# Outer dimensions of two kinds of head copies in an attention and MoE kernel: query rows in 24, 24 and 8, skewed bias rows 32 by 3

## The chip, the cores and the metric

The kernel runs on one core of one Trainium2 chip. The metric is the device time of one execution in microseconds (us). The five compute engines are TensorE (PE; PEld is its weight load), VectorE (DVE), ScalarE (ACT), GpSimd (POOL) and SyncE (SP), which here only issues DMA transfers and waits for semaphores. The core's transfers run on 16 DMA engines.

## The reference, cut to what matters

Two attention blocks in a row and a mixture of experts, on 2 sequences of 1024 tokens with 128 features, 16 heads of 8. The first attention block adds a bias that depends only on the distance i - m (a table of 2L - 1 numbers per head):

```python
q, k, v = (heads(q_), heads(k_), heads(v_))
bias = tisa_bias(kernel_offsets, kernel_amplitudes, kernel_sharpness, l)   # scores[:, i - j + l - 1]
logits = jnp.einsum('bhld,bhmd->bhlm', q, k) * scale + bias[None]
out = jnp.einsum('bhlm,bhmd->bhld', softmax(logits), v)
```

The second one (`_msa`) is the same without the bias, with other weights and after a layer norm. Then come a projection, a top-1 choice among 8 experts and the expert's two matrices.

## The kernel before, in words

**Units.** A stage (0: with the bias, 1: without) is 32 units, a unit being one head of one sequence, 1024 x 1024 scores. Each unit is computed twice. Form A (`block_a`, L1110) has the queries on the partitions, 8 blocks of 128 x 1024; DVE takes each row's maximum, in stage 0 with the bias added from a table in SBUF (L831), in stage 1 without (L834). Form B (`scores_b`, L1166) has the keys on the partitions, so that the exponential (ACT, L693) can go straight into the product with v (`weigh_v`, L1118). The negated maxima enter form B as three more rows of its operand. In stage 0 the bias enters form B through matmuls with a flip matrix (`bias_b`, L1173), which turns around and sums 96 shifted copies of the head's bias row: three bf16 parts by 32 shifts. Form A runs two units ahead of form B (AU = 2), woven into it on PE.

**Operands.** The float32 numbers of q and k are kept as three bf16 parts. q_parts and k_parts lie in DRAM; for each head `rows_of` (L385) copies 56 rows of q and 56 of k (the products of parts that count) into a ring of four head slots, once for each half of the partitions (f = 0, 1). A q copy (L392) reads the same 24 rows twice into 48 partitions; its source has the outer dimension 2. A k copy reads 16 rows, each three times; its source has the outer dimension 16. Eight more rows follow each (L394). `skew_of` (L332, issued at L336) copies the 96 shifted bias rows of a head; its source has the outer dimension 3. `table_of` (L326, L330) copies the bias table of form A, 64 rows at a time.

**The way of the maxima.** For each unit: DVE maxima of 8 blocks, split by POOL into three parts (L561), transposed by PE (L1147), copied by DVE into max_rows (L841), stored by SP to DRAM (`maxima_of`, L418: 24 rows, 6 KB), and after the store has landed loaded as 3 rows into the q ring (L422, two transfers). PE waits for these loads (`mrow_loaded`, L1195) ahead of the unit's first form B block. All of this is SP's queue, written by hand in `stage` (L425): per unit the table, the maxima of the next unit, then at an even unit the skewed copies of the next head (L440) and the q rows of a head to come (L446), at an odd unit its k rows. In the first 8 units of stage 1 two transfers of expert weights follow each (L406, L407).

**Start of a stage.** `first_rows` (L397) stores the parts of sequence 0, loads head 0's rows of it, stores those of sequence 1, waits until all stores have landed (L383) and loads the rest; then come head 1's rows (L413). In stage 0 ACT issues the skewed copies of heads 0 and 1 (L680) meanwhile.

Of the kernel before, what the change touches and what calls it, by code (L numbers as in the profile page):

```python
# [6 lines left out]
def sandwich_kernel(nc, x, w_in, offsets, amplitudes, sharpness, ln1_w, ln1_b, w_qkv, w_proj,  # L7
# [16 lines left out]
    B, L, D = x.shape  # L24
    P = 128
    T = B * L
# [3 lines left out]
    DH = D // H  # L30
    SCALE = float(np.float32(1.0) / np.sqrt(np.float32(DH)))
    EPS = 1e-5
    E, _, HID = w1.shape
    HC = HID // P
    U = B * H
# [5 lines left out]
    PAIRS = H // 2  # L41

    KR = 7 * DH
    QK_DMAS = 8
    HP = P // 2
    UB = 8
    TAW = 2 * L - P
    SKW = 2 * L - 32
# [17 lines left out]
    with ExitStack() as ctx:  # L66
# [265 lines left out]
        def skew_of(queue, h, slot):  # L332

            row = bp_dram[bass.ds(h, 1), 0, 0:SKW]
            src = bass.AP(row.tensor, row.offset, [[2 * L, 3], [1, 32], [1, SKW]])
            queue.dma_start(skew[0:96, slot, 0:SKW], src).then_inc(skew_loaded[slot], 16)  # L336

        ctx.enter_context(nc.allow_non_contiguous_dma(reason="head rows and skewed tables"))
# [4 lines left out]
        def _(sp):  # L343
# [41 lines left out]
            def rows_of(a, h, slot, loaded, which=(0, 1), lo=0, hi=T):  # L385
                for s in which:
                    ring = (q_ring, k_ring)[s][slot]
                    one = (qp_dram, kp_dram)[s][a][bass.ds(h, 1), 0, 0, lo:hi]
                    pairs = ([[0, 2], [T, 3 * DH]], [[T, 2 * DH], [0, 3]])[s]
                    last = (qp_dram[a][bass.ds(h, 1), :, 0, lo:hi], kp_dram[a][bass.ds(h, 1), 2, :, lo:hi])[s]  # L390
                    for f in range(2):
                        sp.dma_start(ring[f * HP:f * HP + 6 * DH, lo:hi],  # L392
                                     bass.AP(one.tensor, one.offset, pairs + [[1, hi - lo]])).then_inc(loaded, 16)
                        sp.dma_start(ring[f * HP + 6 * DH:f * HP + KR, lo:hi],  # L394
                                     last.rearrange("o d n -> (o d) n")).then_inc(loaded, 16)

            def first_rows(a):  # L397

                store_parts(a, range(G // 2))
                rows_of(a, 0, 0, first_loaded[a], lo=0, hi=L)  # L400
                store_parts(a, range(G // 2, G))
                rows_of(a, 0, 0, qk_loaded[a][0], lo=L, hi=T)
# [8 lines left out]
            sp.wait_ge(ones_ready, 1)  # L411
            first_rows(0)
            rows_of(0, 1, 1, qk_loaded[0][1])  # L413
            def maxima_of(a, u, ul):

# [63 lines left out]
        def _(pool):  # L479
            steps = [0]  # L480

            def chain(ins):

                steps[0] += 1
                ins.then_inc(pool_step, 1)
                pool.wait_ge(pool_step, steps[0])
# [6 lines left out]
                                          pattern=[[-1, P]], channel_multiplier=1))  # L493
# [5 lines left out]
                                          pattern=[[P, 2], [-NK, VM]], channel_multiplier=1))  # L499
            nc.gpsimd.affine_select(out=amp_sel[:], in_=amp_sel[:], compare_op=ALU.is_ge, fill=0.0,  # L500
                                    base=NK - 1, pattern=[[-P, 2], [NK, VM]], channel_multiplier=-1).then_inc(mask_ready, 1)
# [9 lines left out]
            chain(nc.gpsimd.memset(flip[:], 0.0))  # L511
            for n in range(3):
                chain(nc.gpsimd.affine_select(out=flip[:], in_=flip[:], compare_op=ALU.not_equal, fill=1.0,
                                              base=-31 - 32 * n, pattern=[[1, 32]], channel_multiplier=1))
            pool.sem_inc(flip_ready, 1)

            nc.gpsimd.iota(order[:], [[-1, E]], base=E, channel_multiplier=0,
# [6 lines left out]
                                          pattern=[[1, P]], channel_multiplier=-1))  # L524
# [3 lines left out]
                                          pattern=[[1, E], [-1, E]], channel_multiplier=0))  # L528
# [95 lines left out]
        def _(act):  # L624
# [54 lines left out]
            for h in range(2):  # L679
                skew_of(act, h, h)  # L680
# [364 lines left out]
        def _(pe):  # L1045
# [90 lines left out]
            def block_a(a, u, ul, qb, guard, halves=(0, 1)):  # L1136

                if guard:
                    pe.wait_ge(max_done[a], QB * u + qb - 1)
                for f in halves:  # L1140
                    ins = scores_a(qb % 2, (ul // B) % 4, ul % B, qb, f)
                return ins
# [34 lines left out]
            def stage(a):  # L1177
                for qb in range(QB):
                    if qb == 0:
                        pe.wait_ge(first_loaded[a], 16 * QK_DMAS)  # L1180
                    block_a(a, 0, 0, qb, qb >= 2).then_inc(sa_done[a], 1)
                pe.wait_ge(qk_loaded[a][0], 16 * QK_DMAS)
                for qb in range(QB):
# [6 lines left out]
                def body(i, first=False, last=False):  # L1190
                    for ul in range(UB):
# [6 lines left out]
                        for kb in range(QB):  # L1198
                            if kb == 0 and lu % B == 0 and not done:
                                pe.wait_ge(qk_loaded[a][(lu // B) % 4], 16 * QK_DMAS * (i + 1 + lu // UB))  # L1200
                            for f in range(2):
# [180 lines left out]
```

## Time and profile before

| | |
|---|---|
| Three runs, median (lowest to highest) | 1099.91 us (1099.27 to 1103.8) |
| The profiled execution, its own time | 1094.4 us |
| Its span, from the first to the last instruction | 1092.3 us |
| PE, DVE, ACT busy | 80%, 71%, 59% of the span |
| Mean granted TensorE clock | 0.906 of full speed (2.4 GHz) |
| DMA: mean rate, reads from HBM | 66 GB/s, 59.95 MB |
| Chain that ended last, by engine | PE 49%, DMA 20%, DVE 9%, ACT 8% |

The span is divided so: the start until about 93 us; stage 0's units until about 558 us; layer norms and projections until about 609 us; stage 1's units until about 968 us; the mixture of experts to the end. The chain is the chain of waits that ended last, followed back from the end: a share of it that belongs to a transfer is time in which nothing else on the chain could go on.

### The profile page before, as it was taken

How to read it: one execution, taken by the hardware profiler on the slowest of the kernel's cores; microseconds unless marked ns; L12 is line 12 of the kernel's file. 1: busy time of each engine (PE TensorE's matmuls, PEld its weight loads, DVE VectorE, ACT ScalarE, POOL GpSimd, SP SyncE). 2: the span in 40 equal slices, each digit the busy share in tenths (PEclk: the TensorE clock that was granted, in tenths of full speed). 3: DMA queues.
4: the chain of work that ended last, by engine and by line, in shares of the span. 5: the costliest groups of instructions: out<-in, count | busy, mean ns of one | idle time of the engine just before them, and what ended most of it. 6: DMA issues, size and time to landing. Idle time of an engine off the chain costs nothing.

```text
span 1092.3 us, 25373 instructions
## 1 busy us (share of the span) xinstructions
PE 870.8 (80%) x9075; PEld 327.7 (30%) x9075; DVE 771.5 (71%) x1388; ACT 641.3 (59%) x1208; POOL 138.9 (13%) x376
## 2 busy tenths in 40 slices
PE   3328979998998999989946387999979999984871
PEld 2102323333332333323313011222322222243861
DVE  7356757776775777767358676899969999746544
ACT  6204646665665666656646066889869889941222
POOL 8100000000000000000010000000100100001772
PEclk9757989999998999999978588999989999996996
DMA  2722223233223223320002323321111110001123
GB/s 56 215 75 74 75 73 86 83 86 87 67 71 80 86 84 84 84 78 24 3 1 62 122 57 89 110 82 48 54 37 48 58 44 30 3 1 48 43 48 89
DMA packets 41965, 72.18 MB, mean 66 GB/s; under 512 B 9177, under 2 KB 28825, under 8 KB 41849
## 3 DMA queue, kind: packets, MB, share of 16 engines
q1 hardware_dynamic: 40018, 65.81, 21.3%
q0 software_dynamic: 1472, 3.02, 1.1%
q10 hardware_dynamic: 358, 1.76, 0.5%
q8 instruction: 79, 1.29, 0.5%
q14 instruction: 38, 0.30, 0.1%
HBM read 59.95 MB, written 10.62 MB: 65 GB/s over the span
## 4 chain that ended last, share of the span: by engine, by line
PE 49%; DMA 20%; DVE 9%; ACT 8%; issue 6%; SPq 4%; POOL 3%; DVEq 0%; ACTq 0%; POOLq 0%
PE bank L1118 16%; DMA maxima_rows<-max_rows 13%; PE bank L1166 13%; PE bank L1173 9%; ACT prob_mem L693 7%; PE bank L1110 6%; DVE unit_max L834 2%; DMA k_parts<-prob_mem 2%; POOL moe_out L616 2%; DMA q_rows<-maxima_rows 2%; DVE stats L750 2%; POOL prob_mem L605 1%; DVE norm L764 1%; SPq L392 1%; SPq L373 1%
## 5 line engine op out<-in xcount | busy, mean ns | idle before, releaser
L693 ACT ACTIVATE prob_mem<-bank 128x512 f32<-128x512 f32 x1024 | 555.3, 597 | 317.7 <-PE bank L1173 232.4
L831 DVE CUSTOM_DVE_ANT_0 y_res<-bank,tables 128x1024 bf16<-128x1024 f32 x256 | 312.3, 1224 | 158.6 <-PE bank L1110 149.5
L834 DVE TENSOR_REDUCE unit_max<-bank 128x1 f32<-128x1024 f32 x256 | 294.7, 1214 | 40.1 <-PE bank L1110 39.9
L1118 PE MATMUL bank<-prob_mem,v_ring 128*32 128x256 f32 x4096 | 315.2, 394 | 2.3 <-issue 1.7
L1110 PE MATMUL bank<-k_rows,q_rows 56*128 56x512 bf16 x512 | 164.0, 425 | 57.9 <-DMA k_rows<-k_parts 43.6
L1166 PE MATMUL bank<-q_rows,k_rows 59*128 59x512 bf16 x512 | 170.3, 401 | 44.8 <-DMA q_rows<-maxima_rows 26.2
L1166 PE MATMUL bank<-more_rows 59*128 59x512 bf16 x512 | 162.3, 389 | 28.2 <-DMA more_rows<-maxima_rows 15.1
L1173 PE MATMUL bank<-feat,flip 96*32 96x512 bf16 x2048 | 163.9, 395 | 0.0
L1110 PE MATMUL bank<-more_rows 56*128 56x512 bf16 x512 | 162.7, 392 | 0.0
L1118 PEld LDWEIGHTS bank<-prob_mem,v_ring 128*32 128x32 f32 x4096 | 107.1, 111 | 150.1 <-ACT prob_mem L693 58.7
L561 POOL CAST max_parts<-unit_max 128x8 bf16<-128x8 f32 x64 | 12.2, 191 | 809.6 <-DVE unit_max L831 463.5
L1166 PEld LDWEIGHTS bank<-q_rows,k_rows 59*128 59x128 bf16 x512 | 39.1, 94 | 167.7 <-ACT prob_mem L693 74.3
L1166 PEld LDWEIGHTS bank<-more_rows 59*128 59x128 bf16 x512 | 39.3, 93 | 147.9 <-ACT prob_mem L693 76.0
L1110 PEld LDWEIGHTS bank<-k_rows,q_rows 56*128 56x128 bf16 x512 | 36.8, 95 | 73.2 <-issue 27.2
L1173 PEld LDWEIGHTS bank<-feat,flip 96*32 96x32 bf16 x2048 | 32.3, 95 | 75.0 <-issue 75.0
L727 ACT ACTIVATE prob_mem<-bank 128x512 f32<-128x512 f32 x23 | 13.8, 598 | 67.5 <-PE bank L1327 67.5
L1110 PEld LDWEIGHTS bank<-more_rows 56*128 56x128 bf16 x512 | 37.6, 94 | 0.3
L815 DVE RECIPROCAL recip<-bank 128x8 f32<-128x8 f32 x64 | 12.0, 187 | 34.2 <-PE bank L1104 34.2
L605 POOL DMA_INDIRECT prob_mem<-tokens,gather_u x23 | 24.8, 1078 | 59.9 <-DVE gather_u L970 53.2
L1104 PE MATMUL bank<-ident,o_ring 128*128 128x128 f32 x128 | 28.2, 302 | 0.9 <-ACT o_ring L670 0.5
L1327 PE MATMUL bank<-prob_mem 128*128 128x128 f32 x184 | 27.2, 294 | 0.0
L670 ACT COPY o_ring<-bank 128x256 f32<-128x256 f32 x64 | 24.3, 379 | 4.9 <-PE bank L1118 4.7
(159 smaller groups left out, 565.4 us busy)
## 6 DMA issues: line engine op xcount, KB each, us to landing
tables<-bias_rows SPq DMA_DIRECT2D x30, 480.0 KB, 8.5
more_rows<-q_parts SPq DMA_DIRECT2D x32, 192.0 KB
more_rows<-k_parts SPq DMA_DIRECT2D x32, 192.0 KB
q_rows<-q_parts SPq DMA_DIRECT2D x28, 192.0 KB
k_rows<-k_parts SPq DMA_DIRECT2D x28, 192.0 KB
feat<-bias_parts SPq DMA_DIRECT2D x14, 378.0 KB
w_moe<-in_L_ffn_w_dram SPq DMA_DIRECT2D x16, 256.0 KB, 3.8
q_parts<-prob_mem SPq DMA_DIRECT2D x8, 384.0 KB, 3.2
```

The lines of the kernel that those rows point to most:

```text
L605: nc.gpsimd.indirect_dma_start(out=slot_rows[:, j % 4, :], out_offset=None, in_=tokens_dram, in_offset=bass.IndirectOffsetOnAxis(ap=gather ...
L616: nc.gpsimd.indirect_dma_start(out=moe_dram, out_offset=bass.IndirectOffsetOnAxis(ap=token_u[:, j:j + 1], axis=0), in_=slot_y[:, j, :], in ...
L670: nc.scalar.copy(o_ring[:, slot, :], AV).then_inc(o_ready[a], 1)
L693: nc.scalar.activation(prob[:, ul % 2, kb, half * N:(half + 1) * N], b_bank(entry(ul, kb, half)), ACT.Exp).then_inc(exp_done[a], 1)
L831: nc.vector.tensor_tensor_reduce(out=no_use[qb % 2], in0=scores, in1=bias, scale=1.0, scalar=LEAST, op0=ALU.add, op1=ALU.max, accum_out=un ...
L834: nc.vector.tensor_reduce(unit_max[:, slot, qb:qb + 1], scores, AX.X, ALU.max).then_inc(max_done[1], 1)
L1104: ins = nc.tensor.transpose(out[:, half * P:(half + 1) * P], o_ring[:, slot, half * P:(half + 1) * P], ident[:])
L1110: return nc.tensor.matmul(SA[slot][:, f, :], q_ring[head_slot][rows, b * L + qb * P:b * L + (qb + 1) * P], k_ring[head_slot][rows, b * L + ...
L1118: ins = nc.tensor.matmul(AV[VM * c:VM * (c + 1), :], v_ring[:, head_slot, b * QB + kb, :], prob[:, ul % 2, kb, c * W:(c + 1) * W], start=( ...
L1166: return nc.tensor.matmul(b_bank(entry(ul, kb, f)), k_ring[ul // B][rows, b * L + kb * P:b * L + (kb + 1) * P], q_ring[ul // B][rows, b * ...
L1173: ins = nc.tensor.matmul(b_bank(entry(ul, kb, f))[32 * c:32 * (c + 1), :], flip[:], skew[0:96, (ul // B) % 2, at:at + N], start=False, sto ...
L1327: ins = nc.tensor.matmul(bank[:, 2 + n % 2, c * P:(c + 1) * P], w_ring[:, n, c * P:(c + 1) * P], slot_feat[:, n, :], start=True, stop=True)
```

## The change

The copies move the same bytes from the same rows to the same partitions, apart from the skewed bias.

- A q copy of 48 rows from a source of 2 by 24 rows is now two copies of 24 rows, whose source has the outer dimension 24. The copy of 8 rows stays (outer dimension 8). A head's rows are therefore 10 transfers and not 8 (`QK_DMAS`).
- The skewed copies read 32 by 3 and not 3 by 32 rows: partition 3 i + n now holds shift i of part n, where partition 32 n + i did. It is one transfer as before.
- The flip matrix has its ones where the new partitions want them.

```diff
-    QK_DMAS = 8
+    QK_DMAS = 10
...
             row = bp_dram[bass.ds(h, 1), 0, 0:SKW]
-            src = bass.AP(row.tensor, row.offset, [[2 * L, 3], [1, 32], [1, SKW]])
+            src = bass.AP(row.tensor, row.offset, [[1, 32], [2 * L, 3], [1, SKW]])
             queue.dma_start(skew[0:96, slot, 0:SKW], src).then_inc(skew_loaded[slot], 16)
...
-                    pairs = ([[0, 2], [T, 3 * DH]], [[T, 2 * DH], [0, 3]])[s]
                     last = (qp_dram[a][bass.ds(h, 1), :, 0, lo:hi], kp_dram[a][bass.ds(h, 1), 2, :, lo:hi])[s]
                     for f in range(2):
-                        sp.dma_start(ring[f * HP:f * HP + 6 * DH, lo:hi],
-                                     bass.AP(one.tensor, one.offset, pairs + [[1, hi - lo]])).then_inc(loaded, 16)
+                        if s == 0:
+                            for r in range(2):
+                                sp.dma_start(ring[f * HP + 3 * DH * r:f * HP + 3 * DH * (r + 1), lo:hi],
+                                             bass.AP(one.tensor, one.offset, [[T, 3 * DH], [1, hi - lo]])).then_inc(loaded, 16)
+                        else:
+                            sp.dma_start(ring[f * HP:f * HP + 6 * DH, lo:hi],
+                                         bass.AP(one.tensor, one.offset, [[T, 2 * DH], [0, 3], [1, hi - lo]])).then_inc(loaded, 16)
...
-                                              base=-31 - 32 * n, pattern=[[1, 32]], channel_multiplier=1))
+                                              base=-93 - n, pattern=[[3, 32]], channel_multiplier=1))
```

How SP's queue stands at an even unit of stage 0 (more_rows and q_rows are slots of the q and k rings, feat holds the skewed copies). Before:

```order
L418 DMA maxima_rows<-max_rows 24x128
L422 DMA q_rows<-maxima_rows 3x512 x2
L336 DMA feat<-bias_parts 96x1x2016
L392 DMA q_rows<-q_parts 48x1x2048
L394 DMA q_rows<-q_parts 8x2048
L392 DMA q_rows<-q_parts 48x1x2048
L394 DMA q_rows<-q_parts 8x2048
L330 DMA tables<-bias_rows 64x1920
L418 DMA maxima_rows<-max_rows 24x128
```

And with the change (its file has four more lines, so L418 is L422 there):

```order
L422 DMA maxima_rows<-max_rows 24x128
L426 DMA q_rows<-maxima_rows 3x512 x2
L336 DMA feat<-bias_parts 96x1x2016
L393 DMA q_rows<-q_parts 24x2048 x2
L398 DMA q_rows<-q_parts 8x2048
L393 DMA q_rows<-q_parts 24x2048 x2
L398 DMA q_rows<-q_parts 8x2048
L330 DMA tables<-bias_rows 64x1920
L422 DMA maxima_rows<-max_rows 24x128
```

Between two stores of maxima SP issues two more transfers, with the same neighbours. SP's queue at the start of a stage, from the first half of head 0's rows to the second. Before:

```order
L392 DMA q_rows<-q_parts 48x1x1024
L394 DMA q_rows<-q_parts 8x1024
L392 DMA q_rows<-q_parts 48x1x1024
L394 DMA q_rows<-q_parts 8x1024
L392 DMA k_rows<-k_parts 48x1x1024
L394 DMA k_rows<-k_parts 8x1024
L392 DMA k_rows<-k_parts 48x1x1024
L394 DMA k_rows<-k_parts 8x1024
L369 DMA q_parts<-prob_mem 384x1x512
L373 DMA k_parts<-prob_mem 16x8x512 x3
```

And with the change:

```order
L393 DMA q_rows<-q_parts 24x1024 x2
L398 DMA q_rows<-q_parts 8x1024
L393 DMA q_rows<-q_parts 24x1024 x2
L398 DMA q_rows<-q_parts 8x1024
L396 DMA k_rows<-k_parts 48x1x1024
L398 DMA k_rows<-k_parts 8x1024
L396 DMA k_rows<-k_parts 48x1x1024
L398 DMA k_rows<-k_parts 8x1024
L369 DMA q_parts<-prob_mem 384x1x512
L373 DMA k_parts<-prob_mem 16x8x512 x3
```

Here too there are two more q transfers ahead of the k rows and ahead of the stores that follow; nothing else changes its place.

## Rows read from the trace of the kernel before

**Rows 1.** The page, part 4: the chain of waits by line.

```profile
PE bank L1118 16%; DMA maxima_rows<-max_rows 13%; PE bank L1166 13%; PE bank L1173 9%; ACT prob_mem L693 7%; PE bank L1110 6%; DVE unit_max L834 2%; DMA k_parts<-prob_mem 2%; POOL moe_out L616 2%; DMA q_rows<-maxima_rows 2%; DVE stats L750 2%; POOL prob_mem L605 1%; DVE norm L764 1%; SPq L392 1%; SPq L373 1%
```

**Rows 2.** Chain of waits, stage 0: start us, us, what.

```profile
257.30 8.79 DMA maxima_rows<-max_rows
...
266.40 1.44 DMA more_rows<-maxima_rows
```

**Rows 3.** PE in order of time, the unit after that store: start, us, instruction, idle before.

```profile
268.16 0.38 PE L1166 MATMUL bank<-more_rows 59*128 59x512 bf16 x1 [2.55 <-DMA more_rows<-maxima_rows]
```

**Rows 4.** Windows there: stretch, us, busy per engine, PEclk, DMA share, GB/s.

```profile
256.00:264.00 8.00, 7.48 (x99) 2.62 (x97) 6.00 (x12) 4.85 (x10) 0.00 (x0) 1.00 0.13 53
...
269.00:271.00 2.00, 2.00 (x18) 0.51 (x12) 1.23 (x2) 1.09 (x2) 0.00 (x0) 0.50 0.79 185
```

**Rows 5.** SP in order of time, issues of that head: start, us to issue, transfer.

```profile
245.90 0.81 SPq L336 DMA_DIRECT2D feat<-bias_parts  x1
246.93 0.69 SPq L392 DMA_DIRECT2D q_rows<-q_parts  x1
...
250.20 0.54 SPq L330 DMA_DIRECT2D tables<-bias_rows  x1
257.30 0.31 SPq L418 DMA_DIRECT2D maxima_rows<-max_rows  x1
...
275.09 0.31 SPq L418 DMA_DIRECT2D maxima_rows<-max_rows  x1
276.39 0.56 SPq L422 DMA_DIRECT2D more_rows<-maxima_rows  x2
```

**Rows 6.** DMA of 511 to 523 us, a skewed copy alone: GB/s in 40 slices of 0.3 us.

```profile
GB/s 0 0 3 7 10 0 0 27 13 27 54 81 81 81 81 81 81 81 135 81 81 81 81 81 67 54 0 0 0 0 0 0 0 0 27 0 27 0 0 0
```

**Rows 7.** SP in order of time, stores of the maxima in stage 0.

```profile
122.00 0.30 SPq L418 DMA_DIRECT2D maxima_rows<-max_rows  x1
...
318.69 0.31 SPq L418 DMA_DIRECT2D maxima_rows<-max_rows  x1
...
339.09 0.31 SPq L418 DMA_DIRECT2D maxima_rows<-max_rows  x1
...
496.30 0.30 SPq L418 DMA_DIRECT2D maxima_rows<-max_rows  x1
...
509.76 0.29 SPq L418 DMA_DIRECT2D maxima_rows<-max_rows  x1
...
523.23 0.30 SPq L418 DMA_DIRECT2D maxima_rows<-max_rows  x1
```

**Rows 8.** PE in order of time, first instruction of stage 0's unit 16.

```profile
330.94 0.60 PE L1166 MATMUL bank<-q_rows,k_rows 59*128 59x512 bf16 x1 [3.55 <-issue]
```

**Rows 9.** Chain of waits, start of stage 0.

```profile
50.46 16.44 DMA k_parts<-prob_mem
...
79.29 5.93 DMA maxima_rows<-max_rows
```

**Rows 10.** Windows of the start of stage 0, columns as in rows 4.

```profile
50.00:52.00 2.00, 0.00 (x0) 0.00 (x0) 0.00 (x0) 0.00 (x0) 0.00 (x0) 0.50 1.06 363
...
52.00:58.00 6.00, 2.80 (x10) 0.47 (x10) 4.13 (x7) 0.00 (x0) 0.00 (x0) 0.50 0.26 91
58.00:64.00 6.00, 1.88 (x8) 0.31 (x6) 5.12 (x10) 0.00 (x0) 0.56 (x4) 0.50 0.19 75
```

**Rows 11.** SP in order of time, stage 1.

```profile
633.73 0.29 SPq L418 DMA_DIRECT2D maxima_rows<-max_rows  x1
...
641.80 0.42 SPq L407 DMA_DIRECT2D w_moe<-in_L_ffn_w_dram  x1
...
740.43 0.30 SPq L418 DMA_DIRECT2D maxima_rows<-max_rows  x1
...
750.18 0.30 SPq L418 DMA_DIRECT2D maxima_rows<-max_rows  x1
```

**Rows 12.** Chain of waits, stage 1, a store of maxima in its first units.

```profile
645.12 6.95 DMA maxima_rows<-max_rows
```

## The prediction

> **What bounds the kernel now.** I read the page first: the chain of waits by line. Among the matmuls stands a transfer, the store of the maxima, with 13% of the span, more than any other transfer [rows 1]. It moves 6 KB, so its time is a wait behind something. Next the chain in time: the store issued at 257.30 lands after 8.79 us, its load takes 1.44 us more [rows 2], and PE, which stood idle for 2.55 us, starts the unit at 268.16 [rows 3]. The store after it, issued at 275.09, lets SP go on at 276.39, after 1.30 us [rows 5]. So the same store takes 1.3 us on an empty queue and 8.8 on a full one.
>
> What fills the queue is seen in the windows. From 256 to 264 us the DMA engines are 13% busy and move 53 GB/s [rows 4]: 0.13 of 16 is two engines, 27 GB/s each. What was issued before were the skewed copies and the q rows of a head [rows 5]. Where the skewed copy runs alone, the rate stands at 81 GB/s from 514.3 to about 518.5 us, slice after slice [rows 6]: three engines of 27. Two is the outer dimension of the q copy's source and three that of the skewed copy's. So a copy here runs on as many engines as its source has outer entries, and the store, some of whose rows go through the same engines, waits until these two or three have finished, while 13 stand idle. Per head the two busiest get 378/3 = 126 KB of skewed rows, 2 x 192/2 = 192 KB of q rows, and some 40 KB of the 8-row copies and the table: about 360 KB, 13.5 us at 27 KB per us. From 247 us on that is 260.5, and later while the table shares them; the landing was at 266.1.
>
> The last piece is the price of the stall. PE has no slack in stage 0: with nothing in the way a unit takes 13.47 us (509.76 to 523.23) [rows 7]. After the idle time the granted clock is 0.50, the lower of the two levels (1.2 GHz), in the window from 269 to 271 us [rows 4]. The stall of 2.55 us plus the slow matmuls make the step 257.30 to 275.09 17.8 us long [rows 5], 4.3 above a clean one.
>
> **The change part by part.** The sum is made against the profiled execution's 1094.4 us (its span of 1092.3 and 2.1 around it).
>
> *1. Stage 0's units, gain 29 us.* From the store at 122.00 to that at 496.30 lie 25 units in 374.3 us [rows 7]; at 13.47 they would take 336.8. The excess is 37.5 us. Ahead of unit 16, the first after the loop's back edge, PE is idle for 3.55 us and waits for nothing that the profile shows ("issue") [rows 8]; that step, 318.69 to 339.09 [rows 7], is 6.9 over, and I leave all of it. That leaves 30.6 in twelve heads, all in the units after a heavy burst. With the change the burst (378 + 448 + 480 = 1306 KB, the table among it) is spread. The nearest rate for such copies on all engines is the 185 GB/s at 0.79 share of k rows and table [rows 4]: 7.1 us from 247, done by 255, before the store at 257.3. The store then lands in 1.3 us, as at 275.09. PE was ready for the unit 2.55 us before 268.16, at 265.6 [rows 3], so store and load may take 8.3 us together; they would take some 3.3. Even at half the rate the burst ends at 261 and PE doesn't wait. I take 29 of the 30.6, for the odd step that stays long. Bounds: 0 (nothing spreads) and 31.
>
> *2. Start of stage 0, gain 10 us.* The last store of k parts, issued at 50.46, takes 16.44 us [rows 9], and SP waits for it. From 50 to 52 us all engines are busy at 363 GB/s, but from 58 to 64 us only 0.19 of them, again three, at 75 [rows 10]: ACT's two skewed copies, 252 KB on each of three engines, and then two engines of q rows. What was still to move after 52 us is the 546 and 450 KB of the two windows behind it and a rest, about 1.1 MB; at between 185 and 363 GB/s that is 3 to 6 us, so the store lands at about 58.5 and not at 66.9, 8.4 us earlier (two more q issues ahead of it, 1.4 us, are in that). Unit 1's rows are issued next: two more q issues cost 1.4 us there, and rows that spread land sooner by about as much (96 KB of 2-KB rows on each of two engines were 3.6 us at 27 KB per us): net nothing. The maxima's first store, 5.93 us [rows 9], falls to about 1.5; DVE's maxima of unit 1 then end last, and about 2 us of the 4.4 show. 8.4 + 2 = 10.4, taken as 10. Bounds 3 and 13.
>
> *3. Start of stage 1, loss 1 us.* There no skewed copy lies in the way, and the stores of the parts wait for SP's own issuing. Two more in each half of the rows cost 4 x 0.69 [rows 5] = 2.8 us; shorter landings give back about 1.8. Bounds: loss 3, gain 2.
>
> *4. Stage 1's first units, gain 13 us.* A clean unit takes 9.75 us (740.43 to 750.18). From 633.73 to 740.43 there are nine in 106.7 us [rows 11], 18.9 over nine clean ones. The store at 645.12 takes 6.95 us there [rows 12]. The q rows (192 KB on each of two engines, 7.3 us) are the tail of each burst at an even unit. With q, k and two expert transfers spread evenly, 1.4 MB or so, the burst takes some 7.6 us at 185 GB/s, about what SP takes to issue it, and the store behind it lands in 2 to 3 us. Some of the excess is the low clock after the stage's start. I take 13. Bounds 5 and 18. Later stage 1 steps are clean already: nothing.
>
> *5. Issue cost, nothing in the loops.* 0.69 us for each of two more transfers per head [rows 5], 1.4 us. In stage 0 SP is done with the table at 250.7 and waits for the maxima until 257.30 [rows 5]: 6.6 us of cover. In stage 1's first units it ends at 642.22 [rows 11] with the next store at 645.12 [rows 12]: 2.9. Only there would a shorter unit (9.75) bring SP near the path. The flip matrix costs nothing: the same three POOL instructions at the start, the same 32 columns for PE.
>
> One rule bears on how far a 24-row copy spreads, for which no row stands; the rates above bound it between two engines and all, and I take many, by the fit of both rates to the outer dimension. The Trainium skill (DMA: Bandwidth & Descriptors, in the section on why a DMA increments its semaphore by 16 and not by 1) says that a DMA takes the largest number up to 16 that divides the slowest dimensions of both sides: 2 and 3 here before, as the trace agrees with 54 and 81 GB/s, and 12 and 16 with the change; 12 or 16 makes no difference to the sum. No copy with 24 outer entries is seen alone in this trace.
>
> Sum: 29 + 10 - 1 + 13 = 51 us, 1094.4 - 51 = 1043.4. The three runs' median is 5.5 above the profiled execution; a measurement is compared with the median, so I give 1099.9 - 51 = 1048.9, or 1049. The sum's bounds together (0 and so on up, but hardly all at one end) give 1037 to about 1075.
>
> **The rivals.**
>
> *A. The q rows stay on few engines, only the skewed copies spread.* This would come from the two 24-row copies running one behind the other on the same engines, so that splitting wins nothing. For it: no row shows a 24-row q copy. Against it: the rates fit the outer dimension twice. Then engines 0 and 1 have 360 - 126 + 24 = 258 KB, 9.6 us from 247: free by about 257 to 259, and the store still lands in time, so term 1 stays at 27. Term 2 falls to 7, term 4 to 0, term 3 to -3: 1099.9 - 31 = 1069. The Trainium skill has a rule that points this way (same page, Rules for kernel authors: two transfers to disjoint partition halves serialize, so one should not bother). Its reason is that both halves already use all 16 engines, which the 53 GB/s of the before trace denies here. Chance 0.1.
>
> *B. The reads of the skewed copies collide.* Its 96 rows overlap, shifted by 2 bytes, and 16 engines would read the same few kilobytes at once. The table, also overlapping, is among what moves at 185 GB/s, half of the 363 seen elsewhere. If the skewed copy alone fell to some 50 GB/s it would take 7.6 us and the burst about 13, until 260: the stalls shrink but some stay. Term 1 then gives 20, term 2 gives 5: 1099.9 - 37 = 1063. Chance 0.09.
>
> *C. Slower: SP's issuing becomes the path.* The place is the queue between the loads of the maxima (L422) and the next store (L418). If the split copies cost much more to issue than 0.69 us (queue space, 24 entries over more engines), the store starts late in every even unit. It decides from 6.6 us more per head in stage 0 and about 3 in stage 1; at 4 us an issue (two more, and four dearer) stage 1 would lose some 10 us per head, 100 us, against 40 gained: 1160. Even at a mild 2 us an issue stage 1 loses about 3 x 16 = 48 and the result is 1050 + 60 = 1110. Against it: the table copy, with 2.5 times the bytes of a q copy, costs 0.54 us and not more [rows 5]. Chance 0.03.
>
> *D. No change.* The spread copies reach the store just as late, since the sum of bytes and not the two engines is the limit: 1306 KB would have to take over 13 us, below 100 GB/s. The 185 GB/s of the nearest window speaks against it. 1098. Chance 0.03.
>
> **How the numbers follow.** My forecast has 0.75, A 0.1, B 0.09, C 0.03, D 0.03. The forecast, A and B are all faster by more than 0.5% (5.5 us, about what a measurement of this kernel can tell from no change): 0.94. D is 0.03, C 0.03. The range holds the time 8 times in 10: from 1036, where all terms of the forecast come near their upper bounds (31 + 13 + 0 + 18 = 62, 1038), to 1072, which takes in A and B.
>
> **What would show it right or wrong.** In the profile after: the chain's share of the maxima's store falls from 13% to 2 or 3%; the steps between stores in stage 0 are all 13.4 to 13.6 us but for unit 16; right after a skewed copy the windows show a share above 0.7 for 5 to 7 us and none at 0.13; the mean granted clock rises above 0.93; the k parts' store at the start takes 7 to 9 us and not 16.4; stage 1's first stores of the maxima land within 3.5 us. It is wrong if the 0.13 windows stay (A), if a window with the skewed copy alone shows a high share at a low rate (B), or if the store is issued late behind SP's other transfers (C). If the stores land quickly but the steps stay at 15 us or more, PE's stall had another cause and the theory of terms 1 and 4 falls.

## The result and the profile after

The changed kernel takes 1032.59 us (median of 4 runs, 1031.16 to 1035.85) against 1099.59 (1097.62 to 1103.8): a ratio of 0.939, 95% interval 0.9354 to 0.9426, 67 us less. The forecast was 1049, with 1036 as the low end. So the sign and the mechanism were right and the size was not: a quarter of the gain wasn't foreseen.

The profiled execution has a span of 1030.0 us (before 1092.3) and a mean granted clock of 0.923 (before 0.906). The chain by line on the page of the changed kernel, which answers to [rows 1] (its line numbers are four higher from L418 on):

```profile
PE bank L1122 21%; PE bank L1170 16%; PE bank L1177 13%; ACT prob_mem L697 10%; PE bank L1114 7%; PE bank L1341 1%; PE bank L1331 1%; PE bank L1108 1%; DVE stats L754 1%; DVE norm L768 1%; DVE unit_max L838 1%; DMA prob_mem<-tokens,gather_u 1%; ACT o_ring L674 1%; DVE meanvar L757 1%
```

The maxima's store, 13% of the chain before, is gone from the list. SP's queue at an even unit of stage 0, in order of time (start us, us to issue), which answers to [rows 5]:

```profile
133.54 0.30 SPq L422 DMA_DIRECT2D maxima_rows<-max_rows  x1
134.84 0.55 SPq L426 DMA_DIRECT2D more_rows<-maxima_rows  x2
135.44 0.58 SPq L336 DMA_DIRECT2D feat<-bias_parts  x1
136.06 1.52 SPq L393 DMA_DIRECT2D q_rows<-q_parts  x2
...
139.05 0.51 SPq L330 DMA_DIRECT2D tables<-bias_rows  x1
147.01 0.30 SPq L422 DMA_DIRECT2D maxima_rows<-max_rows  x1
```

And the windows over it (stretch, us, busy per engine, PEclk, DMA share, GB/s), which answer to [rows 4]:

```profile
137.00:139.00 2.00, 2.00 (x32) 0.75 (x24) 1.72 (x3) 1.57 (x4) 0.00 (x0) 1.00 0.85 245
139.00:141.00 2.00, 2.00 (x28) 0.67 (x28) 1.50 (x4) 1.39 (x3) 0.00 (x0) 1.00 0.86 195
141.00:143.00 2.00, 2.00 (x36) 0.80 (x28) 1.65 (x3) 1.25 (x3) 0.45 (x3) 1.00 1.00 160
143.00:145.00 2.00, 2.00 (x30) 0.71 (x24) 1.72 (x3) 1.63 (x4) 0.30 (x2) 1.00 0.22 46
145.00:147.00 2.00, 1.50 (x17) 0.45 (x15) 1.71 (x6) 1.34 (x4) 0.00 (x0) 1.00 0.00 0
```

The same bytes go through in some 8 us, most of them with nearly all engines busy, and nothing is left when the store is issued at 147.01; before, two engines worked on for 8 us more. The skewed copy alone, on the changed kernel from 466 to 478 us (GB/s in 40 slices of 0.3 us, and the issue), answers to [rows 6]:

```profile
GB/s 0 0 0 10 10 0 0 134 81 202 390 390 94 0 0 0 0 55 0 0 0 0 0 0 0 0 0 0 0 0 0 0 0 0 0 27 0 27 0 0
...
feat<-bias_parts SPq DMA_DIRECT2D x1, 378.0 KB, 3.6
```

What took over 4 us at 81 GB/s now takes some 1.8 us (six slices) with 390 GB/s at its height. The stores of stage 0, which answer to [rows 7]:

```profile
106.61 0.30 SPq L422 DMA_DIRECT2D maxima_rows<-max_rows  x1
...
282.46 0.31 SPq L422 DMA_DIRECT2D maxima_rows<-max_rows  x1
...
302.71 0.31 SPq L422 DMA_DIRECT2D maxima_rows<-max_rows  x1
...
451.56 0.29 SPq L422 DMA_DIRECT2D maxima_rows<-max_rows  x1
```

From the fourth store to the 29th it is 344.95 us, before 374.3. The step 282.46 to 302.71 is the one at the loop's back edge, 20.25 us as before (20.40). Of the other 24 steps 22 are 13.40 to 13.47 us and two 14.25. The start, which answers to [rows 9]:

```profile
58.59 0.72 SPq L393 DMA_DIRECT2D q_rows<-q_parts  x2
...
69.14 0.30 SPq L422 DMA_DIRECT2D maxima_rows<-max_rows  x1
70.79 0.92 SPq L426 DMA_DIRECT2D q_rows<-maxima_rows  x2
...
80.25 0.29 SPq L422 DMA_DIRECT2D maxima_rows<-max_rows  x1
```

SP goes on from the stores of the parts at 58.59, before at 66.9; the first maxima go out at 69.14, before at 79.29, and SP goes on to their loads after 1.65 us and not 5.95. Last stage 1, which answers to [rows 11], with the last store of all:

```profile
575.64 0.30 SPq L422 DMA_DIRECT2D maxima_rows<-max_rows  x1
585.06 0.29 SPq L422 DMA_DIRECT2D maxima_rows<-max_rows  x1
...
673.73 0.30 SPq L422 DMA_DIRECT2D maxima_rows<-max_rows  x1
683.49 0.30 SPq L422 DMA_DIRECT2D maxima_rows<-max_rows  x1
...
885.30 0.29 SPq L422 DMA_DIRECT2D maxima_rows<-max_rows  x1
```

The places to compare in the kernel before are these (the others stand in [rows 7] and [rows 11]):

```profile
621.10 0.30 SPq L418 DMA_DIRECT2D maxima_rows<-max_rows  x1
...
952.37 0.29 SPq L418 DMA_DIRECT2D maxima_rows<-max_rows  x1
```

So the span's 62.3 us divide: to the fourth store 122.00 - 106.61 = 15.4; stage 0's 25 steps 29.4; from there to stage 1's first store (621.10 and 575.64) 124.8 - 124.1 = 0.7; the next ten steps (621.10 to 740.43 against 575.64 to 673.73) 119.3 - 98.1 = 21.2; the rest of stage 1 0.4; and from the last store to the end it is 144.7 against 139.9, 4.8 us lost.

Of the signs that the prediction named, the stall's all came: the store has left the chain, the steps of stage 0 are clean, and SP waits at most 2.5 us for a store of the maxima in stage 1's first ten steps. One didn't: the mean granted clock was to rise above 0.93 and is 0.923. In the changed kernel it is 0.99 from 107 to 452 us and 0.98 from 674 to 885 us; most of what is left of the slow clock lies ahead of the units (0.80 until 69 us), between the stages (0.83) and behind the last store (0.82), where the change does little.

### The profile page after: what moved, and what is told of

It is laid out like the page before. It is cut to its first block, busy times and chain, and to the rows that moved or that the text cites. A ratio compares the mean times of both kernels' runs of the same rounds, so it can differ in the third digit from the quotient of the medians.

```text
span 1030.0 us, 25473 instructions
## 1 busy us (share of the span) xinstructions
PE 859.8 (83%) x9075; PEld 329.0 (32%) x9075; DVE 769.7 (75%) x1388; ACT 640.3 (62%) x1208; POOL 138.8 (13%) x376
## 3 DMA queue, kind: packets, MB, share of 16 engines
q10 hardware_dynamic: 384, 1.76, 0.6%
q8 instruction: 78, 1.28, 0.5%
## 4 chain that ended last, share of the span: by engine, by line
PE 64%; ACT 12%; DVE 6%; issue 5%; DMA 2%; SPq 1%; another core or an unknown queue 1%; POOL 1%; DVEq 0%; ACTq 0%; POOLq 0%
PE bank L1122 21%; PE bank L1170 16%; PE bank L1177 13%; ACT prob_mem L697 10%; PE bank L1114 7%; PE bank L1341 1%; PE bank L1331 1%; PE bank L1108 1%; DVE stats L754 1%; DVE norm L768 1%; DVE unit_max L838 1%; DMA prob_mem<-tokens,gather_u 1%; ACT o_ring L674 1%; DVE meanvar L757 1%
## 5 line engine op out<-in xcount | busy, mean ns | idle before, releaser
L1122 PE MATMUL bank<-prob_mem,v_ring 128*32 128x256 f32 x4096 | 310.0, 388 | 2.5 <-issue 2.0
L1170 PE MATMUL bank<-q_rows,k_rows 59*128 59x512 bf16 x512 | 167.4, 395 | 18.5 <-ACT prob_mem L697 8.9
L1170 PE MATMUL bank<-more_rows 59*128 59x512 bf16 x512 | 159.5, 384 | 12.7 <-ACT prob_mem L697 9.4
L1177 PE MATMUL bank<-feat,flip 96*32 96x512 bf16 x2048 | 161.1, 389 | 0.0
L1114 PE MATMUL bank<-more_rows 56*128 56x512 bf16 x512 | 158.7, 382 | 0.0
L1331 PE MATMUL bank<-prob_mem 128*128 128x128 f32 x184 | 28.4, 304 | 6.6 <-issue 6.0
L1341 PE MATMUL bank<-prob_mem 128*128 128x128 f32 x184 | 26.4, 290 | 4.2 <-issue 2.3
```

The costliest lines, as they stand in the source:

```text
L1114: return nc.tensor.matmul(SA[slot][:, f, :], q_ring[head_slot][rows, b * L + qb * P:b * L + (qb + 1) * P], k_ring[head_slot][rows, b * L + ...
L1122: ins = nc.tensor.matmul(AV[VM * c:VM * (c + 1), :], v_ring[:, head_slot, b * QB + kb, :], prob[:, ul % 2, kb, c * W:(c + 1) * W], start=( ...
L1170: return nc.tensor.matmul(b_bank(entry(ul, kb, f)), k_ring[ul // B][rows, b * L + kb * P:b * L + (kb + 1) * P], q_ring[ul // B][rows, b * ...
L1177: ins = nc.tensor.matmul(b_bank(entry(ul, kb, f))[32 * c:32 * (c + 1), :], flip[:], skew[0:96, (ul // B) % 2, at:at + N], start=False, sto ...
L1331: ins = nc.tensor.matmul(bank[:, 2 + n % 2, c * P:(c + 1) * P], w_ring[:, n, c * P:(c + 1) * P], slot_feat[:, n, :], start=True, stop=True)
L1341: ins = nc.tensor.matmul(bank[:, 4 + n % 2, 0:D], hidden[:, n % 2, c, :], w_ring[:, n, HID + c * D:HID + (c + 1) * D], start=(c == 0), sto ...
```

## The experiments

"Theory T" is the prediction's: a copy runs on as many engines as its source has outer entries, and the maxima's store waits for the busiest of the engines that it shares. The rivals are S (what counts is into how many transfers the q rows are cut) and what the expectations call theory B (the skewed copies are all of it; not the rival B of the prediction). Kernels that were timed together share their runs of the kernel before: its median is 1102.77 us for e1 to e4 and 1102.54 for e6, e7, e9 and e10.

**e1, the skewed copies alone.** The q copies are as before.

```diff
-            src = bass.AP(row.tensor, row.offset, [[2 * L, 3], [1, 32], [1, SKW]])
+            src = bass.AP(row.tensor, row.offset, [[1, 32], [2 * L, 3], [1, SKW]])
...
-                                              base=-31 - 32 * n, pattern=[[1, 32]], channel_multiplier=1))
+                                              base=-93 - n, pattern=[[3, 32]], channel_multiplier=1))
```

> The skewed copies read 32 by 3 rows, the q copies stay as in the kernel before (48 rows, outer dimension 2). Theory T (a copy runs on as many engines as its source has outer entries; the maxima's store waits for the busiest of its engines): with the skewed rows spread, engines 0 and 1 carry about 258 KB per head, 9.6 us, and are free at about the time of the store, so stage 0's units between its fourth and 29th store come close to the changed kernel (345 to 352 us where before has 374), the start gains about 8 us, stage 1's first units gain nothing (ten steps 119 us, as before). Sum about 35 us: 1060 to 1068. Theory S (the number of transfers into which the q rows are cut is what counts, not the engines): no gain beyond a few us, 1090 or more. Theory B (the skewed copies are all of it, q nothing): 1033.

Measured: 1072.04 us (1066.33 to 1072.69), ratio 0.9698 (0.9633 to 0.9762). Stage 0 is nearly as clean as with the whole change:

```profile
113.57 0.30 SPq L418 DMA_DIRECT2D maxima_rows<-max_rows  x1
...
465.02 0.29 SPq L418 DMA_DIRECT2D maxima_rows<-max_rows  x1
...
589.70 0.30 SPq L418 DMA_DIRECT2D maxima_rows<-max_rows  x1
...
711.03 0.30 SPq L418 DMA_DIRECT2D maxima_rows<-max_rows  x1
```

351.45 us for the 25 steps, 6.5 more than with the change, all of it in the first two (16.39 and 17.14). The two stores there take 9.51 and 8.62 us. Ahead of the first, q and k rows of a head are issued in one unit (from 105.73 us on); ahead of the second, SP, held up by the first, issues the skewed copy and the q rows only from 123.69 on, 6.3 us before the store. Stage 1's first ten steps take 121.3 us, nothing gained. There the windows show the two engines again:

```profile
616.00:618.00 2.00, 2.00 (x28) 0.53 (x24) 2.00 (x2) 1.96 (x5) 0.00 (x0) 1.00 0.13 51
```

Both are what T says; the total is 4 us above its range. S, which expected 1090 or more, and B, which expected 1033, both miss.

**e2, the q copies alone.** The skewed copies and the flip matrix are as before.

```diff
-            src = bass.AP(row.tensor, row.offset, [[1, 32], [2 * L, 3], [1, SKW]])
+            src = bass.AP(row.tensor, row.offset, [[2 * L, 3], [1, 32], [1, SKW]])
...
-                                              base=-93 - n, pattern=[[3, 32]], channel_multiplier=1))
+                                              base=-31 - 32 * n, pattern=[[1, 32]], channel_multiplier=1))
```

(against the changed kernel)

> The q copies as in the change, the skewed copies and the flip matrix as before (outer dimension 3). T: three engines carry about 126 + 56 KB and more of k, 7 us per head, so stage 0's units are as with the whole change (345 us from the fourth store to the 29th); at the start ACT's two skewed copies still hold three engines for 9.4 us, and the last k parts store lands at about 62 us (66.9 before, 58.6 with the change); stage 1 is as with the change (98 us for ten steps). 1034 to 1042. If the skewed copies were needed too, stage 0 would stay above 360 us and the time above 1048. B: 1090 or more.

Measured: 1035.96 us (1035.65 to 1036.36), ratio 0.9385 (0.9329 to 0.9441).

```profile
58.25 0.71 SPq L393 DMA_DIRECT2D q_rows<-q_parts  x2
...
74.08 0.30 SPq L422 DMA_DIRECT2D maxima_rows<-max_rows  x1
...
113.28 0.30 SPq L422 DMA_DIRECT2D maxima_rows<-max_rows  x1
...
458.29 0.29 SPq L422 DMA_DIRECT2D maxima_rows<-max_rows  x1
```

345.01 us in stage 0 and 98.55 for stage 1's ten steps: as the whole change. The one thing off is the start. The parts' stores let SP go on at 58.25, not at 62 as expected, and the loss comes later, where unit 1's rows are loaded: the first maxima go out 15.8 us after that, with the whole change 10.6. Theory B falls: the q copies alone give nearly all of the gain. The two halves of the change don't add up: against the same runs of the kernel before they gain 31 and 67 us alone, and both together 70 to 72 (e3 and e4 below, which are the changed kernel). In stage 0 removing either burden is nearly enough (351.45 and 345.01 us for the 25 steps, with both removed 344.95, before 374.3).

**e3 and e4, meant as outer dimension 2 and 8.**

```diff
-                                             bass.AP(one.tensor, one.offset, [[T, 3 * DH], [1, hi - lo]])).then_inc(loaded, 16)
+                                             bass.AP(one.tensor, one.offset, [[12 * T, 2], [T, 12], [1, hi - lo]])).then_inc(loaded, 16)
```

(e4: `[[3 * T, 8], [T, 3], [1, hi - lo]]`)

> The changed kernel, but each 24-row q copy reads its rows as 2 by 12: same bytes, same number of transfers as the change, outer dimension 2. T: the q rows are back on two engines, so this is as the skewed copies alone (e1), 1060 to 1070, with windows at 0.13 DMA share and about 54 GB/s in stage 1. S: splitting is what counts, 1033. The issue of a copy: if a third dimension makes it dear, a 24-row copy takes about 0.6 us and not 0.35.

> The changed kernel, but each 24-row q copy reads its rows as 8 by 3: outer dimension 8. T: eight engines carry 48 KB each of a head's q rows, under 2 us, so nothing waits: 1033, or up to 1037 if three dimensions make each issue 0.6 us and not 0.35 (eight such issues more or dearer at each start of a stage, about 1 us per half of the rows). S: 1033. If only 12 or more engines would do, 1040 and more.

Measured: 1031.16 us (1029.05 to 1032.87), ratio 0.9346 (0.9289 to 0.9404), and 1032.59 (1032.35 to 1038.88), ratio 0.9372 (0.9309 to 0.9435). Taken at its word e3 would have ended T. Their traces agree: two of their q copies are mostly issued in 0.70 to 0.72 us, as in the change, where e6's take some 1.3 to 1.5. One thing is worth reading in them, the windows from 80 to 86 us, first of the changed kernel:

```profile
80.00:86.00 6.00, 5.90 (x76) 2.12 (x80) 3.92 (x9) 3.67 (x7) 0.00 (x0) 1.00 0.36 95
```

and of e4, the same program:

```profile
80.00:86.00 6.00, 6.00 (x50) 1.67 (x48) 2.47 (x4) 2.18 (x5) 0.00 (x0) 0.53 0.32 94
```

At the granted clock of 0.53, close to the lower level, e4's second step takes 15.78 us, that of the changed kernel 13.26. The difference is one between executions of the same program, not one that the change makes.

**e6, a true outer dimension of 2.**

```diff
-                                             bass.AP(one.tensor, one.offset, [[T, 3 * DH], [1, hi - lo]])).then_inc(loaded, 16)
+                                             bass.AP(one.tensor, one.offset, [[T, 2], [2 * T, 12], [1, hi - lo]])).then_inc(loaded, 16)
```

 Here each 24-row q copy reads the even rows and then the odd ones, 2 by 12, which can't be merged: outer dimension 2, the same two transfers per half as the change, skewed copies spread. Its q rows stand in another order than the k rows, so the scores are other numbers; all work is the same. T (engines by outer dimension): as e1, 1062 to 1075, ten first steps of stage 1 near 121 us where the change has 98, windows at 0.13 share there. S (splitting is what counts): 1031 to 1036.

Measured: 1072.34 us (1071.95 to 1074.03), ratio 0.9733 (0.968 to 0.9785), the time of e1. Stage 1's first ten steps take 120.9 us. A window, a store in the chain of waits, and SP's issue of two of the new copies:

```profile
620.00:622.00 2.00, 2.00 (x24) 0.43 (x20) 2.00 (x3) 1.95 (x5) 0.00 (x0) 1.00 0.13 52
```

```profile
631.67 8.80 DMA maxima_rows<-max_rows
```

```profile
608.36 1.34 SPq L393 DMA_DIRECT2D more_rows<-q_parts  x2
```

The q rows are cut into just as many transfers as in the change, and all of q's gain is gone. S falls. (The scores that e6, e7 and e10 compute are other numbers than the kernel's; behind their last store they take 144.2 to 146.1 us, e1 145.4, so the difference lies in the units.)

**e7, one transfer of 48 rows with outer dimension 24.**

```diff
-                            for r in range(2):
-                                sp.dma_start(ring[f * HP + 3 * DH * r:f * HP + 3 * DH * (r + 1), lo:hi],
-                                             bass.AP(one.tensor, one.offset, [[T, 3 * DH], [1, hi - lo]])).then_inc(loaded, 16)
+                            sp.dma_start(ring[f * HP:f * HP + 6 * DH, lo:hi],
+                                         bass.AP(one.tensor, one.offset, [[T, 3 * DH], [0, 2], [1, hi - lo]])).then_inc(loaded, 16)
```

(and `QK_DMAS = 8`)

> One q copy of 48 rows per half as before (8 transfers per head), but its source is 24 rows, each read twice in a row: outer dimension 24, inner 2. The q rows stand in another order than the k rows, so the scores are other numbers. Skewed copies spread. T: as the change, 1030 to 1036, since only the outer dimension matters. S: as e1, 1062 to 1075. Issue cost: if it goes with the rows of a copy and not with its number of engines, 0.6 to 0.7 us, as two of 24.

Measured: 1034.08 us (1031.9 to 1035.56), ratio 0.9376 (0.9324 to 0.9428): the changed kernel's. Stage 1's first ten steps take 98.2 us. The window and the issue:

```profile
622.00:624.00 2.00, 2.00 (x25) 0.47 (x18) 2.00 (x3) 2.00 (x6) 0.98 (x5) 1.00 1.00 242
```

```profile
610.43 0.84 SPq L392 DMA_DIRECT2D q_rows<-q_parts  x1
```

With e6 this is the decisive pair: split and outer dimension 2 gains nothing, unsplit and outer dimension 24 gains all. The further dimension in the source, which e6 and e7 both have, is no explanation either.

**e10, outer dimension 4.** As e6 with `[[T, 4], [4 * T, 6], [1, hi - lo]]`.

> As e6, but 4 by 6 rows: outer dimension 4, the q rows in another order than k's. T: four engines carry 96 KB each per head, 3.6 us and not 7.3; of what e6 loses in stage 1's first ten steps (about 23 us) at most a third is left, stage 0 as the change: 1033 to 1043, and above all between e7 and e6. S: 1031 to 1036.

Measured: 1043.76 us (1043.32 to 1045.47), ratio 0.9473 (0.9423 to 0.9524); ten steps take 102.0 us, and a store there in the chain is

```profile
615.20 5.15 DMA maxima_rows<-max_rows
```

So stage 1's first ten steps are 120.9, 102.0 and 98.2 us with 2, 4 and 24 outer entries. An outer dimension of 4 leaves a sixth of the loss. That these copies run on four engines is inferred from this; no window shows them alone. The total is 1 us above the range expected. Of its 9.4 us over e7's profile 3.8 lie in these ten steps, 2.8 and 2.5 at the starts of the stages and 2.2 behind the loop's back edge in stage 0, and 1.9 come back behind the last store; whether the dearer issues cause those outside the ten steps wasn't tried apart.

**e9, e11, e12, e14: what the start is worth.** ACT's two skewed copies and head 1's table are issued early and stand ahead of the parts' stores. e9 issues them when head 0's rows have landed:

```diff
-            for half in range(2):
-                table_of(act, 1, 1, half)
             act.wait_ge(bias_parts_stored, 16 * 4)
+            act.wait_ge(qk_loaded[0][0], 16 * QK_DMAS)
             for h in range(2):
                 skew_of(act, h, h)
+            for half in range(2):
+                table_of(act, 1, 1, half)
```

> The changed kernel, but ACT issues the two skewed copies and then head 1's table only when head 0's rows have all landed. T for the start: the last k parts store waits behind whatever is in the queues (1.7 MB of tables and skewed rows before it), so it lands 3 to 5 us earlier than at 58.6 and the first maxima's store goes out 2 to 5 us earlier than at 69.1; the skewed rows are still there when form B wants them: 1028 to 1031 against 1032.6. Rival: unit 0's and 1's blocks on DVE set the start, and the late skewed copies are waited for: 1033 to 1037.

Measured: 1037.71 us (1033.53 to 1040.02), ratio 0.9401 (0.9345 to 0.9456).

```profile
52.89 0.71 SPq L393 DMA_DIRECT2D q_rows<-q_parts  x2
...
63.35 0.30 SPq L422 DMA_DIRECT2D maxima_rows<-max_rows  x1
74.57 0.92 SPq L426 DMA_DIRECT2D q_rows<-maxima_rows  x2
...
83.28 0.29 SPq L422 DMA_DIRECT2D maxima_rows<-max_rows  x1
```

The stores land 5.7 us earlier and the first maxima go out 5.8 us earlier, but these now wait 11.2 us behind tables and skewed rows. The theory of the expectation, an earlier end, falls. The time is 0.7 us above the rival's range, but neither of the rival's reasons is what the trace shows: DVE's blocks don't hold up the first store (it goes out 5.8 us earlier), and PE waits 9.35 us for the load of the maxima, not for the skewed copies. The bytes that were put later came back on the maxima's store. e11 keeps the table early and has only the skewed copies wait for the parts' stores; e12 puts the table behind the first maxima's loads:

```diff
             act.wait_ge(bias_parts_stored, 16 * 4)
+            act.wait_ge(parts_stored[0], 16 * 4 * G)
             for h in range(2):
                 skew_of(act, h, h)
```

> The changed kernel, but ACT issues its two skewed copies only when all stores of the parts have landed; head 1's table stays early. In e9 the stores landed at 52.9 and not at 58.6, but table and skewed rows together then held up the first maxima's store by 11.2 us. Theory (the stores wait for the bytes ahead of them): 0.76 MB less ahead of them, so they land at 55 to 57, the first maxima's store goes out 2 to 3 us earlier than at 69.1 and still lands in 2 to 3 us: 1029 to 1032 against 1032.6. Rival (any byte put later comes back on the maxima's store): 1032 to 1036.

> As e11, and head 1's table is issued only when the first maxima have been loaded. Theory: stores land at about 53, the first maxima's store goes out at about 63.5 and lands in 2 to 3 us, form B starts about 5 us earlier; the table is there when form A's unit 2 wants it (it takes about 4 us): 1026 to 1030. Rival: DVE waits for the table, or the clock's rise later than with the change takes the gain: 1031 to 1036.

Measured, on another chip on which the kernel before takes 1092.59 us: 1024.51 (1023.16 to 1026.59), ratio 0.9389 (0.9353 to 0.9425), and 1026.03 (1024.9 to 1029.48), ratio 0.9406 (0.9369 to 0.9443). The times look better than the change, the ratios don't. So both were set side by side: the changed kernel (e13) and e11 again (e14).

> The changed kernel itself beside e14 on one chip, since kernels timed on different chips can't be compared within 1% (before took 1102.5 and 1092.6 us in the last two comparisons). 0.935 to 0.942 of before.

> e11 again, beside the changed kernel. If the earlier stores are worth anything at the end, 1 to 4 us below e13; rival (what the start gains is given back by the clock, which rises later: in e11 the second step was 16.1 us and not 13.3): within 1 us of e13.

Measured: 1026.1 us (1024.48 to 1027.46), ratio 0.9381 (0.934 to 0.9423), and 1025.21 (1020.89 to 1029.63), ratio 0.9375 (0.933 to 0.942). No difference that can be told. In e14 SP goes on at 54.31 and not at 57.94, the first maxima go out at 66.98 and not at 68.50, and at the third store 0.7 us are left (93.84 against 94.54). The first loss is in the k rows for which form A's next blocks wait. They now share the queue with the skewed copies, which is the likely reason, though no run takes the two apart. e13, then e14:

```profile
64.03 1.03 PE L1114 MATMUL bank<-k_rows,q_rows 56*128 56x512 bf16 x4 [4.92 <-DMA k_rows<-k_parts]
```

```profile
62.51 1.03 PE L1115 MATMUL bank<-k_rows,q_rows 56*128 56x512 bf16 x4 [3.62 <-DMA k_rows<-k_parts]
```

So 1.5 of 3.6 us are left there, and 0.8 of them goes in the second step (15.75 us, in e13 14.93), as e14's rival said. In e12 the rival's reason holds as well: SP goes on at 53.97, but the first maxima go out at 67.02 and not at 63.5, and in the step behind them, 14.42 us and not 11.11, DVE waits for the table that was put later:

```profile
77.53 1.23 DVE L837 CUSTOM_DVE_ANT_0 y_res<-bank,tables 128x1024 bf16<-128x1024 f32 x1 [4.83 <-DMA tables<-bias_rows]
```

No version here beats the change.

## Why the prediction was right, and where not

**What failed.** The mechanism was right; two terms of the sum were too small. Term 4, stage 1's first units, was put at 13 us and gave 21.2. Term 2, the start of stage 0, was put at 10 and gave 15.4. Both went over their upper bounds, 18 and 13, and with 1.7 us in term 3 they took the time to 1032.59, below the low end of 1036.

**The mechanism held at each point where it was tested.** These are the gain by outer dimension and not by number of transfers (e6, e7, e10), the store behind the busiest engine, and the order in which the windows, the chain and the clock changed. One count in it was loose: by the bytes on the two busiest engines the store of [rows 2] would have landed at 260.5, and it landed at 266.1. That the engines were shared with the table meanwhile is argued and not measured. The rule that the prediction cites from the Trainium skill (DMA: Bandwidth & Descriptors, in the section on why a DMA increments its semaphore by 16 and not by 1) agrees with the runs as far as they can tell: 2 and 4 outer entries are slow and less slow, 24 and 32 are not. The rule in that page's Rules for kernel authors, that two transfers to disjoint partition halves serialize, so that one should not bother, did not decide here. e6 is such a split and gains nothing, as the rule has it, but not for the page's reason that all 16 engines are in use already, since its window stands at 0.13. What gained was the outer dimension.

**Term 1, stage 0's units: 29 forecast, 29.4 measured.** What I left in it also stayed: the step of unit 16 is 6.8 us over a clean one.

**Term 2, the start: 10 forecast, 15.4 measured.** The 8.4 us of the parts' stores were right (8.3). The rest was mis-sized in three places. Unit 1's rows stood at net nothing: from the landing of the parts' stores to the first maxima's store it was 12.4 us before and is 10.6 now, 1.8 less, and in e6, whose q copies have the outer dimension 2, it is 12.5. The first maxima's store and load were thought half hidden, 2 us, and gave 3.3 in the step behind them (14.39 before, 11.11 now). The last 2.0 us are the second step, 15.23 before and 13.26 now, and in part luck. The granted clock there stood at 0.50 from 93.68 to 96 us before, and at 1.00 from 80.25 to 82 us now; in repeats of the same program the step is 13.27 (e3), 14.93 (e13) and 15.78 (e4). With e4's trace the start's gain is 13.1.

**Term 3, start of stage 1: 1 us lost forecast, 0.7 gained between the two stores.** From the first store of the parts (589.89 and 546.62) to the first maxima's the gain is 2.2 (31.2 before, 29.0 now, 29.2 to 29.3 in the repeats e3, e4 and e13). The other 1.5 went ahead of it, between the 29th store and that one, which takes 95.1 us in the change and in e13 but 93.6 in e3, e4 and before, so it isn't the change's. The step that failed is the price of an issue, 2.8 us. Two 24-row copies are issued there in 0.70 to 0.72 us, as long as one 48-row copy before; I had charged 0.69 for each. Over the whole kernel 50 of the 68 pairs take that, the others up to 1.70. In e6 two copies of 24 rows in three dimensions take 1.28 to 1.76, and in e7 one of 48 rows 0.80 to 0.94. So it was the source's extra dimension that was dear, as far as these copies tell, and not the number of transfers. Rival C had no ground.

**Term 4, stage 1's first units: 13 forecast, 21.2 measured.** Two errors. Of the 18.9 us over clean steps I took 13, leaving 5.9 to the clock after the stage's start and to a burst that would still be in flight. The nine steps are now 88.7 us, 0.9 over: both together cost 0.9. Slow clock that came behind a stall went with the stall, as after this one in the kernel before:

```profile
651.00:654.00 3.00, 0.08 (x2) 0.09 (x4) 0.29 (x1) 0.00 (x0) 0.98 (x5) 1.00 0.03 7
654.00:657.00 3.00, 3.00 (x24) 0.52 (x24) 1.71 (x2) 2.04 (x4) 0.00 (x0) 0.60 0.26 64
```

And the step ahead of the nine, 621.10 to 633.73, stood in no term: it fell from 12.63 to 9.42 us, 3.2 more. SP went on from its store after 6.0 us before and 1.85 now.

**The base.** From its last maxima's store to the end the profiled execution of the kernel before took 139.9 us and that of the changed kernel 144.7, and the change touches nothing there. The traces fall into two groups. In nine of them (the changed kernel, e1 to e4, e6, e7, e9 and e10) it is 142.8 to 146.1 us, and the chain of waits has three to five pieces there, 9.4 to 13.8 us in all, of this kind (in the changed kernel):

```profile
974.50 4.00 another core or an unknown queue
```

In the other five (the kernel before and e11 to e14) it is 137.7 to 139.9 us, and there is no such piece. What these waits are the profile can't name, so that stays open. The 4.8 us lost in the profile don't appear in the medians: 62.3 + 4.8 is the 67 us measured. That the timed executions of the kernel before had the longer end is the reading that fits, since they took 1097.6 to 1103.8 us and the profiled one 1094.4, but no trace shows it.

**The range.** Its low end was the sum of the upper bounds, 62 us with term 3 at nothing, and the terms gave 66.7. The bound of term 4 left out the step before its nine; that of term 2 left out the rows and the clock. Rival A of the prediction (few engines for the 24-row copies) is refuted by the ten steps of stage 1. The 1069 us that it gave for that case were near the mark: e1, where the q copies keep the outer dimension 2, took 1072. B (overlapping reads) is refuted by the 390 GB/s of the skewed copy alone, D by the result.

## What to carry to other kernels

A small transfer that is late while the DMA engines are mostly idle may be waiting for one engine, and not for bandwidth: compare the DMA share in the window before it lands with 1/16, 2/16, 3/16, and look for a copy whose outermost dimension is that small. Turn the access pattern so that a large count stands outside, and check in the built program that it still does. When the stall goes, count the whole excess over a clean step as its gain, the slow clock behind it included (here all but 0.9 of 18.9 us came back), and list every step between two markers, so that none is in no term.

## What was not expected of the hardware

A further dimension in the source made a 24-row copy's issue on SP dearer, 0.67 us against 0.35 (e6 against the change); a 48-row copy with one took 0.69 before and 0.84 in e7, so it isn't the many engines that make an issue cheap. And the kernel before differs by 1% between chips (1092.6 and 1102.5 us), while the ratio of the change to it stays between 0.9346 and 0.939 in four measurements. e11's absolute time, 0.8% below the first one of the change, was no gain at all: of the 7.6 us by which its span is shorter, 6.9 lie behind the last store, where the unnamed waits are missing.
